# Experts of layer 0: routing weight applied behind the down projection, one gelu activation for the gate, first steps interleaved with the first units

## What is computed

```python
x = _layernorm(x + _L0_attn_ref(...))
# _L0_ffn_ref, ALPHA, LIMIT = 1.702, 7.0
logits = x @ router_weight
top_vals, top_idx = jax.lax.top_k(logits, K)            # K = 2
scores = jax.nn.softmax(top_vals, axis=-1)
w = jnp.zeros((T, E), x.dtype).at[jnp.arange(T)[:, None], top_idx].set(scores)
gu = jnp.einsum('th,ehf->tef', x, gate_up_proj) + gate_up_proj_bias
gate = gu[..., ::2]
up = gu[..., 1::2]
gate = jnp.minimum(gate, LIMIT)
up = jnp.clip(up, -LIMIT, LIMIT)
glu = gate * jax.nn.sigmoid(gate * ALPHA)
act = (up + 1.0) * glu
down = jnp.einsum('tei,eih->teh', act, down_proj) + down_proj_bias
out = jnp.einsum('te,teh->th', w, down)
x = _layernorm(x + out)
```

## Time and profile before

| | us |
|---|---|
| median of 3 runs | 876.09 |
| the runs | 876.09, 877.26, 871.70 |
| span of the profiled execution, first to last instruction | 871.1 |

### The profile page before, as it was taken

The page is one execution under the profiler, slowest core; times in us unless marked ns, Lnnn a source line. Parts: engine busy times, 40 slices in busy tenths (PEclk is TensorE's granted clock), DMA queues, the critical chain, the costliest instruction groups (busy, mean ns, idle before and its releaser), DMA issues. The chain is left out here.

```text
span 871.1 us, 18432 instructions
## 1 busy us (share of the span) xinstructions
PE 677.3 (78%) x6663; PEld 420.5 (48%) x6663; DVE 560.3 (64%) x1476; ACT 464.6 (53%) x690; POOL 506.0 (58%) x652
## 2 busy tenths in 40 slices
PE   7747999999768999999986767999996513898400
PEld 3423555555435566666653434766664202555300
DVE  5877888888377977787787662444546884122116
ACT  5434777777655666666654674667663600232102
POOL 7844777767553555555554784666663602787743
PEclk9976999999989999999997996999998755899765
DMA  5764473431000000000002799999990350355344
GB/s 159 245 212 95 126 192 101 120 85 42 3 2 1 1 2 1 1 1 1 1 2 78 235 287 184 199 194 189 186 196 12 107 137 13 75 122 100 34 88 126
DMA packets 134984, 86.04 MB, mean 99 GB/s; under 512 B 11120, under 2 KB 131440, under 8 KB 134768
## 3 DMA queue, kind: packets, MB, share of 16 engines
q1 hardware_dynamic: 128112, 79.57, 38.6%
q0 software_dynamic: 5632, 4.33, 3.8%
q10 hardware_dynamic: 1152, 0.98, 0.4%
HBM read 54.96 MB, written 29.49 MB: 97 GB/s over the span
## 5 line engine op out<-in xcount | busy, mean ns | idle before, releaser
L771 POOL TENSOR_TENSOR m_prod<-m_upc,m_gatec 128x512 f32<-128x512 f32 x64 | 99.5, 1555 | 101.9 <-DVE m_upc L601 101.9
L2161 ACT ACTIVATE a_prob<-a_ps_pair 128x1024 f32<-128x1024 f32 x96 | 93.1, 1024 | 48.2 <-PE a_ps_pair L1997 36.3
L2173 POOL TENSOR_SCALAR_AFFINE_SELECT a_prob<-a_prob 128x512 f32<-128x512 f32 (+1 forms) x96 | 76.5, 804 | 51.1 <-ACT a_prob L2161 50.9
L1832 ACT ACTIVATE a_prob<-a_ps_pair 128x1024 f32<-128x1024 f32 x96 | 96.6, 1024 | 13.2 <-PE a_ps_pair L1635 10.3
L1873 POOL TENSOR_SCALAR_AFFINE_SELECT a_prob<-a_prob 128x512 f32<-128x512 f32 (+1 forms) x96 | 75.5, 787 | 41.2 <-ACT a_prob L1832 40.5
L1771 DVE TENSOR_REDUCE a_mx<-a_ps_pair 128x4 f32<-128x1024 f32 x64 | 77.8, 1220 | 24.3 <-PE a_ps_pair L1676 22.6
L715 ACT ACTIVATE m_gate<-m_ps_g,bgu 128x512 f32<-128x512 f32 x64 | 44.0, 687 | 47.5 <-PE m_ps_g L460 47.5
L460 PE MATMUL m_ps_g<-m_x1T,wgu 128*128 128x512 f32 x128 | 66.2, 599 | 0.0
L1417 ACT ACTIVATE c_hT<-c_ps_x,c_w 128x512 f32<-128x512 f32 x16 | 11.0, 688 | 102.2 <-PE c_ps_x L1236 102.2
L462 PE MATMUL m_ps_u<-m_x1T,wgu 128*128 128x512 f32 x128 | 65.4, 592 | 0.0
L1450 POOL DMA_INDIRECT sum<-c_o,c_idx x32 | 50.4, 1574 | 16.5 <-issue 8.5
(11 more groups left out here) (297 smaller groups left out, 1696.9 us busy)
## 6 DMA issues: line engine op xcount, KB each, us to landing
qst<-scratch_q SPq DMA_DIRECT2D x64, 128.0 KB, 4.0
kst<-scratch_k SPq DMA_DIRECT2D x64, 128.0 KB, 3.9
scratch_q<-p_parts SPq DMA_DIRECT2D x16, 384.0 KB, 2.8
scratch_k<-p_parts SPq DMA_DIRECT2D x16, 384.0 KB, 2.8
...
```

What stands on the lines that cost most here:

```text
L771: nc.gpsimd.tensor_tensor(prod[:, n % 2, :], upc[:, n % 2, :], gatec[:, n % 2, :], ALU.mult).then_inc(s_pr, 1)
L1832: nc.scalar.activation(prob[:, r % 6, :], pair[(0, 2, 1)[j]][:, :], ACT.Exp, scale=scale, bias=0.0).then_inc(s_e, 1)
L2161: nc.scalar.activation(prob[:, r % 6, :], pair[r % 2][:, :], ACT.Square, scale=scale, bias=1.0).then_inc(s_e, 1)
L2173: nc.gpsimd.affine_select(out=blk, in_=blk, compare_op=ALU.is_ge, fill=0.0, base=0, pattern=[[0, n], [1, P]], channel_multiplier=-1).then_ ...
```

## The change

What changes in the stage:

- The routing weight goes behind the down projection. `broadcast`, `sel`, the split into bf16 parts and the sum in PSUM are gone. `reduce` writes each expert's result to one of two banks `ps_n`, and VectorE's new `accumulate` adds weight times result to `xn`, one operation per tile with the weight as a per-partition scalar.
- The down bias is weighted by `add_bias` on TensorE in f32, and added once a chunk by VectorE.
- The gate's bias, tanh, clip and products become one ScalarE activation, `Gelu_apprx_sigmoid`, straight from PSUM. Its result is clipped at the value that the limit 7 gives (`GLU_LIMIT`), in `activate`. GpSimd has no work left in a unit. The softmax over two is written with tanh in place of exp.
- `expand` does the up half first. Scores, transposes and routing steps of the front stand between the first units. The later tiles' routing stands at units 8, 10 and 12.

```diff
+GLU_LIMIT = LIMIT / (1.0 + exp(-ALPHA * LIMIT))
+ABUFS = 3
...
                 def score(c):
                     pe.wait_ge(s_xT, c + 1)
                     after(pe, s_lc, c)
+                    if c > 2:
+                        pe.wait_ge(s_lk, c)
...
+                def add_bias(c):
+                    pe.wait_ge(s_wT, c + 1)
+                    for t in range(4):
+                        here = slice(t * P, (t + 1) * P)
+                        last = nc.tensor.matmul(ps_bias[c % 2][:, here], wT[:, c % 2, here], bd[:, :], start=True, stop=True)
+                    last.then_inc(s_bm, 1)
...
-                    after(pe, s_gb, n - 1)
-                    nc.tensor.matmul(ps_g[n % 2][:, :], wgu[:, e, 0, :], xc, start=True, stop=True).then_inc(s_g, 1)
                     after(pe, s_uc, n - 1)
                     nc.tensor.matmul(ps_u[n % 2][:, :], wgu[:, e, 1, :], xc, start=True, stop=True).then_inc(s_u, 1)
-
-                def broadcast(n):
...
-                    nc.tensor.matmul(ps_w[n % 2][:, :], sel[:, e, :].bitcast(BF16), wTp[:, c % 2, :], start=True, stop=True).then_inc(s_bc, 1)
+                    after(pe, s_gl, n - 1)
+                    nc.tensor.matmul(ps_g[n % 2][:, :], wgu[:, e, 0, :], xc, start=True, stop=True).then_inc(s_g, 1)
...
+                def reduce(n):
+                    e = n % E
+                    pe.wait_ge(s_act, n + 1)
+                    after(pe, s_acc, n - 1)
...
+                        last = nc.tensor.matmul(ps_n[n % 2][:, here], act[:, n % ABUFS, here], wd[:, e, :], start=True, stop=True)
...
+                for n in range(2, units):
+                    if n < NCH:
+                        score(n)
+                    expand(n)
+                    if n < NCH:
+                        turn_score(n)
+                    if n + 2 < NCH:
+                        turn_x(n + 2)
+                    reduce(n - 2)
+                    if n in turn_at:
+                        turn_weights(turn_at.index(n))
+                    if n in bias_at:
+                        add_bias(bias_at.index(n))
...
-                    nc.vector.scalar_tensor_tensor(glu[:, u, :], th[:, u, :], 1.0, prod[:, u, :], ALU.add, ALU.mult).then_inc(s_gl, 1)
+                def activate(n):
                     ve.wait_ge(s_gl, n + 1)
...
+                    ve.wait_ge(s_ucl, n + 1)
+                    after(ve, s_dn, n - ABUFS + 1)
+                    nc.vector.scalar_tensor_tensor(act[:, n % ABUFS, :], glu[:, n % 2, :], GLU_LIMIT, upc[:, n % 2, :], ALU.min, ALU.mult)\
+                        .then_inc(s_act, 1)
+
+                def accumulate(n):
+                    c, e = n // E, n % E
+                    ve.wait_ge(s_dn, n + 1)
+                    ve.wait_ge(s_wt, 1 if c < groups[0][1] else 2)
+                    after(ve, s_acc, n)
+                    after(ve, s_y, biased[0])
+                    for t in range(4):
+                        y = xn[:, 4 * c + t, :]
+                        last = nc.vector.scalar_tensor_tensor(y, ps_n[n % 2][:, t * P:(t + 1) * P], wt[:, 4 * c + t, e:e + 1], y,
+                                                              ALU.mult, ALU.add)
+                    last.then_inc(s_acc, 1)
...
+                for n in range(3, units):
                     c, e = n // E, n % E
                     clip(n)
-                    weigh(n - 1)
+                    if n < NCH:
+                        keep_logits(n)
+                    activate(n)
                     if n == 3:
+                        accumulate(0)
+                        norm.invert_rest(ve, s_inv)
+                        make_shift(slice(norm.early, NTILE))
+                        normalise(7)
+                    accumulate(n - 2)
+                    if n == 8:
                         pick_first(1)
-                    if n == 5:
+                    if n == 10:
                         pick_second(1)
-                    if n == 7:
+                    if n == 12:
                         weigh_picks(1)
-                    if n == 9:
-                        split_weights(1)
...
+                def take_gate(n):
+                    act_e.wait_ge(s_g, n + 1)
+                    after(act_e, s_act, n - 1)
+                    nc.scalar.activation(glu[:, n % 2, :], ps_g[n % 2][:, :], ACT.Gelu_apprx_sigmoid, bias=bgu[:, n % E, 0:1]).then_inc(s_gl, 1)
...
-                        nc.gpsimd.memset(wtp[:, :, :], 0.0).then_inc(s_wz, 1)
-                nc.gpsimd.memset(wTp[:, :, :], 0.0).then_inc(s_wTz, 1)
...
+                        nc.gpsimd.memset(wt[:, :, :], 0.0).then_inc(s_wz, 1)
+                        nc.gpsimd.memset(wT[:, :, :], 0.0).then_inc(s_wTz, 1)
```

More of the change, by code:

```diff
@@ L1 @@
 from contextlib import ExitStack
+from math import exp
 import concourse.bass as bass
@@ L423, in turn_x @@
                     pe.wait_ge(s_x1p, c + 1)
-                    after(pe, s_xT, c - 1)
+                    after(pe, s_xT, c - 1 if c < 4 else c)
+                    if c == 4:
+                        pe.wait_ge(s_lk, 2)
+                    out = ps_n[c % 2] if c < 4 else ps_r
                     for t in range(4):
-                        last = nc.tensor.transpose(ps_w[c % 2][:, t * P:(t + 1) * P], xn[:, 4 * c + t, :], ident[:, :])
+                        last = nc.tensor.transpose(out[:, t * P:(t + 1) * P], xn[:, 4 * c + t, :], ident[:, :])
                     last.then_inc(s_xp, 1)
@@ L528, in _ @@
             def _(ve):
-                done = [0]
+                done, biased = [0], [0]
                 def step(ins):
@@ L583, in weigh_picks @@
+                    done[0] += 1
+                    step(nc.vector.tensor_scalar(p2[:, h, :], d[:, h, :], 0.5, 0.5, ALU.mult, ALU.add))
+                    nc.vector.tensor_tensor(ra[5][:, h, :], ra[1][:, h, :], wide(p1, h), ALU.mult).then_inc(s_rt, 1)
+                    done[0] += 1
                     step(nc.vector.tensor_tensor(ra[4][:, h, :], ra[4][:, h, :], wide(p2, h), ALU.mult))
-                    step(nc.vector.tensor_tensor(wt[:, h, :], ra[5][:, h, :], ra[4][:, h, :], ALU.add))
@@ L677, in _ @@
                         norm_out.refine_early(ve, n - E * (NCH - 1) - 1)
-                weigh(E * NCH - 1)
-                add_residual(NCH - 1)
+                for n in (units - 2, units - 1):
+                    accumulate(n)
                 row_stats(NCH - 1)
@@ L702, in runner_up @@
                     act_e.wait_ge(s_ro, group + 1)
[L703 removed]
+                    nc.scalar.activation(rs[4][:, h, :], rs[4][:, h, :], ACT.Tanh, scale=0.5).then_inc(s_ra, 1)
                 def copy_weights(c):
@@ L707, in copy_weights @@
                     act_e.wait_ge(s_wTz, 1)
-                    after(act_e, s_bc, E * (c - 1))
-                    after(act_e, s_dn, E * (c - 2) + 1)
-                    nc.scalar.activation(wTp[0:32, c % 2, :], ps_sum[c % 2][0:32, 0:CH // 2].bitcast(BF16), ACT.Copy).then_inc(s_wT, 1)
-                def take_gate(n):
-                    act_e.wait_ge(s_g, n + 1)
-                    after(act_e, s_gc, n - 1)
-                    nc.scalar.activation(gate[:, n % 2, :], ps_g[n % 2][:, :], ACT.Identity, bias=bgu[:, n % E, 0:1]).then_inc(s_gb, 1)
+                    after(act_e, s_bm, c - 1)
+                    nc.scalar.activation(wT[0:32, c % 2, :], ps_bias[c % 2][0:32, :], ACT.Copy).then_inc(s_wT, 1)
                 def take_up(n):
@@ L2259 @@
     gu = a["L0_ffn_gate_up_proj"].reshape(E, C, P, 2)
-    half_bf16 = 0x3F00
-    sel = np.zeros((P, E, P), np.uint16)
-    for part in range(3):
-        sel[part * E + np.arange(E), np.arange(E)] = half_bf16
     host.update({
```

261 lines of the change are left out of this document (84 added, 177 removed).

## The result

The changed kernel took 853.7 us (median of 4 runs, 851.28 to 856.66), beside 876.67 for the kernel before on the same chip: a ratio of 0.975, 95% interval 0.972 to 0.978. The forecast was 860.5 with a range of 853 to 869.

The account below looks back on a forecast made before the run. TensorE was taken to bound the kernel's changed stage, before and after. Gains of 9.1 (steady), 5.0 (front) and 1.5 us (tail) sum to 15.6, taking the median from 876.1 to 860.5 us, range 853 to 869.

Parts of the forecast that it names:

- the front: From the stage's first transpose to the start of unit 8 (of 64 chunk-expert units): 5.0 us gain.
- the steady part: From the start of unit 8 to the start of unit 63, TensorE-bound: 165.05 to 155.9 us, 9.1 gain.
- Rival 1: Short accumulations on VectorE don't overlap, each advances 0.34 us, and VectorE just becomes the bound: 869 us, 12%.
- Rival 3: Each accumulation on VectorE costs 0.49 us with no overlap, so the kernel gets slower: 887 us, 5%.
- Rival 2: The stage's start gains nothing because TensorE's half clock holds on longer: 865.5 us, 11%.
- the half clock: TensorE at 1.2 GHz early in the stage; the low clock was to add 2.3 us there.
- the unseen operation: VectorE's new 128x128 accumulation from PSUM with per-partition scalar, shown by no row: 0.34 us long, advancing 0.26.
- the routing of group two: Later tiles' routing on VectorE, units 8 to 12: makes VectorE late, costing TensorE 1.5 us.
- The wait for the logits: TensorE's score(5) waits for VectorE's keep_logits(4), near unit 5: about 3.2 us.
- handovers: First handovers between engines at the stage's start: about 1.5 us.
- Table load: ScalarE loads the new function's table at the first gate: 1.3 us, no drain, hidden beside TensorE's work.
- Tail: From the start of unit 63 to the stage's end: 10.0 us becomes 8.5, gain 1.5.

Follow-up runs that it names:

- experiment 2: The changed kernel with one bf16 128x512 matmul per unit put back on TensorE, its result overwritten: median 865.47 us, ratio 0.989.
- experiment 4: The changed kernel with one more VectorE operation of 128x512 per unit, into a spare tile: median 874.38 us, ratio 1.000.
- experiment 5: The kernel before with the gelu alone, the routing weight still ahead of the down projection: median 870.67 us, ratio 0.996.
- experiment 6: The changed kernel with all transposes, scores and the first group's routing ahead of unit 0: median 861.23 us, ratio 0.984.
- experiment 7: The changed kernel with the gate's old chain (bias, clip, tanh, product) put back, the weight still behind the down projection: median 862.79 us, ratio 0.988.
- experiment 3: The changed kernel with one more VectorE operation of 128x128 per unit, into a spare tile: median 855.79 us, ratio 0.980.

## Why the prediction was right, step by step

**Which resource.** TensorE bounds the steady part, before and after: full in the windows but for 0.11 us, and experiment 2 gives back 0.20 us a unit for 0.2 of work. None of the three rivals came about in the changed kernel. Rival 1 (VectorE draws level) asked for 0.34 of advance in the accumulation; it is 0.26. Rival 3 asked for 0.49 of length; it is 0.343. Rival 2 had the front give nothing because the half clock holds on; it gave 8.5 us, and the clock was 1.00 from 252 us on. The fear had ground, though: in four neighbours of this kernel (experiments 4 to 7) the half clock came back in the front.

**The bound on the unseen operation.** The forecast took 0.34 long and 0.26 apart from a 128-column PSUM row and a pointer on 256 columns. The trace has 0.343 and 0.26, and the room it leaves VectorE is 0.4 us a unit, as experiments 3 and 4 show. The prediction set beside rival 1 a rule of the Trainium skill (VectorE: DVE Perf Modes, "The DRAIN you can't avoid"), by which each would advance by its full length. The same section adds that a next operation that is not held starts earlier, which the prediction left out. The rows agree with that: 1.12 for four of 0.34.

**Steady part.** 155.9 was forecast, 154.4 of work and 1.5 for the routing of group two; 154.27 came. The work is 153.75: 55 steps of 2.61, eight bias groups of 0.89, and seven weight transposes of 0.44, where 0.53 was put. The remaining 0.52 is the routing. VectorE's clip stood 1.8 us behind the start of its unit's expand at unit 8 and 5.0 at unit 14: it fell behind by 3.2 us, close to the 3.5 of the forecast. That reached TensorE at units 15 and 16, whose steps are 0.17 and 0.35 us too long (the accumulation ends at 304.48, the down projection starts at 304.63). So the room was some 2.7 us where 2.3 was taken. With experiment 2's longer steps the hold-up is gone. The gain was too small by 1.6 us: 1.0 from the routing and 0.65 from the transposes.

**Front.** Forecast 35.7 us behind the first transpose, measured 32.2. The wait for the logits was at its place, unit 5, for its reason, and 1.98 in place of 3.2: from `keep_logits(2)` to `keep_logits(4)` VectorE took 10.1 us (258.29 to 268.43) where the sum had 11.5. The work, in start-to-start distances of the changed kernel: transposes 0.44 (forecast 0.53), turned score 0.11, in the first two 0.2 (forecast 0.25), score 0.36 as forecast: 7.3 for eight in place of 9.1. The expands took 0.96 + 0.86, since the up half behind a score is 0.1 longer. With eight of them 14.6, six down projections 5.8 and one weight transpose 0.4 the work is 28.1, near the 28.7 of the forecast, by errors that cancelled. The half clock cost (1.87 - 0.88) + (0.58 - 0.36) + (1.64 - 0.96) = 1.9 where 2.3 was taken. 28.1 + 1.9 + 2.0 = 32.0 leaves 0.2 for handovers, for which 1.5 was put. So the front was too dear by the wait (1.2), the handovers (1.3), the work (0.6) and the clock (0.4).

**Table load.** Forecast 1.3 us without a drain, hidden. ScalarE's timeline after:

```profile
252.24 1.28 ACT L706 ACT_TABLE_LOAD   x1
253.53 0.69 ACT L706 ACTIVATE m_glu<-m_ps_g,bgu 128x512 f32<-128x512 f32 x1
```

The next activation starts 1.29 behind, and TensorE shows no wait there. The drain of about 1.38 us that the Trainium skill adds (ScalarE: Activation LUTs, "What ACT_TABLE_LOAD costs") isn't seen here either.

**Tail.** 8.5 forecast, 8.42 measured. One step in it was not foreseen: the last down projection waited 0.85 us for the accumulation of unit 61, which holds its bank. It stood beside VectorE's own chain, which sets the end and has no wait over 0.2 us from 434 us on, so by these rows it cost little. No run tests that.

**Order of the parts.** The forecast gave the gelu no price of its own. From the kernel before, in the order gelu, weight behind, spread front, the stage lost 1.25, 9.9 and 9.6 us. Two of these kernels ran part of the front at half clock; taking off the estimates of experiments 5 and 6 (2.8 and 6.2 us) the steps would be some 4.1, 13.3 and 3.4. With the gelu last (experiment 7 as the step ahead of it) the first two together are worth 10.4 and the gelu 10.4, or some 11.8 and 9.0 at equal clock. Either way the parts are not additive: the gelu is worth more than twice as much beside the others as alone.

**From the stage to the median.** The stage gained 5.2 us more than forecast. The medians differ by 23.0, 7.4 more than the forecast's 15.6; the remaining 2 lie within the spread outside the stage, whose cause stays open. The measured 853.7 is only 0.7 above the lower bound of 853. The bound allowed for no wait in the front and none at the routing; of these came 2.2 of the 5.2 us. The other 3 came from handovers, TensorE's own work and half clock, which cost less than was put and which the range had not counted. That the bound held is partly luck.
